# Wide attention on one core: another order of TensorE's work within a pair of heads, and one value projection of the next batch in every pair

## The reference, cut to what matters

```python
def _L2_attn_ref(x, Wq, Wk, Wv, Wo, bo):
    q, k, v = (x @ Wq), (x @ Wk), (x @ Wv)            # each to (b, 512, 16, 64)
    bias = slope[:, None, None] * (pos[:, None] - pos[None, :])
    scores = jnp.einsum('bihd,bjhd->bhij', q, k) * scale + bias[None]
    scores = jnp.where(causal[None, None], scores, jnp.float32(-1e+30))
    attn = jax.nn.softmax(scores, axis=-1)
    out = jnp.einsum('bhij,bjhd->bihd', attn, v).reshape(b, n, H * DH)
    return out @ Wo + bo
x = x + _L2_attn_ref(_layernorm(x, axis=-1), ...)
```

## Time and profile before

| | us |
|---|---|
| profiled execution, its own time | 3037.45 |
| its span on the core | 3035.5 |
| median of the runs | 3040.95 |
| TensorE busy | 2375.1 (78%) |
| VectorE busy | 2067.0 (68%) |
| ScalarE busy | 1820.5 (60%) |
| mean granted TensorE clock | 0.867 of 2.4 GHz |

### The profile page before, as it was taken

How to read it: one execution, slowest core, us unless ns; L and a number is a source line. 1 busy time by engine, 2 the same in 40 slices (tenths; PEclk the granted TensorE clock), 3 DMA queues, 4 the chain that set the end, 5 groups by cost and what they waited for, 6 DMA issues and landing times. The chain is left out here.

```text
span 3035.5 us, 44101 instructions
## 1 busy us (share of the span) xinstructions
PE 2375.1 (78%) x13097; PEld 1228.9 (40%) x13097; DVE 2067.0 (68%) x5951; ACT 1820.5 (60%) x4643; POOL 928.2 (31%) x1192
## 2 busy tenths in 40 slices
PE   4645574828888878289999999996767888888887
PEld 4434443612222246244444444443523444444452
DVE  4516651659999947656666666665558999999855
ACT  2111213317777763167677667774438999999964
POOL 2640166254344332200000000000454444444336
PEclk7776676558999975589999999998788999999979
DMA  6320232022424200000000000000011111111000
GB/s 178 70 48 0 84 61 46 1 37 49 77 48 76 51 8 0 29 1 1 1 1 1 1 1 1 1 1 1 1 33 29 29 29 29 29 29 22 8 1 28
DMA packets 230435, 86.72 MB, mean 29 GB/s; under 512 B 175234, under 2 KB 223298, under 8 KB 230210
## 3 DMA queue, kind: packets, MB, share of 16 engines
q1 hardware_dynamic: 215298, 71.60, 11.4%
q0 software_dynamic: 9856, 7.58, 1.9%
q10 hardware_dynamic: 5056, 4.83, 0.6%
HBM read 26.53 MB, written 15.50 MB: 14 GB/s over the span
## 5 line engine op out<-in xcount | busy, mean ns | idle before, releaser
L2183 ACT ACTIVATE s_pT<-s_ps_t 128x512 f32<-128x512 f32 x1024 | 626.5, 639 | 142.6 <-PE s_ps_t L1783 124.9
L1936 DVE TENSOR_REDUCE s_neg_max<-s_ps_a 128x1 f32<-128x512 f32 x1024 | 666.6, 682 | 64.9 <-PE s_ps_a L1749 55.1
L2174 ACT ACTIVATE s_first<-s_ps_a,s_neg_max 128x512 f32<-128x512 f32 x512 | 391.8, 765 | 25.2 <-DVE s_neg_max L1936 23.8
L1795 PE MATMUL s_ps_t<-ident,s_first 128*128 128x128 f32 x2048 | 316.8, 285 | 83.6 <-ACT s_pT L2183 70.8
L2592 ACT ACTIVATE s_e<-s_e,s_neg_max 128x128 f32<-128x128 f32 (+3 forms) x512 | 283.2, 555 | 164.9 <-DVE s_neg_max L2492 162.6
L139 POOL TENSOR_TENSOR s_rstd<-s_ve,minus_half 128x4 f32<-128x4 f32 x48 | 50.6, 1054 | 1001.5 <-DVE s_ve L126 1000.8
L2105 POOL TENSOR_SCALAR s_first<-s_first,s_rec 128x512 f32<-128x512 f32 x128 | 232.5, 1816 | 368.3 <-DVE s_rec L1942 362.4
L2492 DVE CUSTOM_DVE_ANT_0 s_e<-s_ps_a,w_alibi 128x128 f32<-128x128 f32 (+3 forms) x512 | 230.5, 488 | 113.7 <-PE s_ps_a L2362 113.7
L1749 PE MATMUL s_ps_a<-s_lanesT 64*128 64x512 bf16 x1024 | 274.9, 400 | 40.1 <-DMA s_lanesT<-n_lanes 23.4
L1795 PEld LDWEIGHTS s_ps_t<-ident,s_first 128*128 128x128 f32 x2048 | 220.9, 142 | 183.3 <-ACT s_pT L2183 142.0
L1810 PE MATMUL s_ps_o<-s_pT,n_v_pad 128*32 128x512 f32 x2048 | 277.6, 616 | 12.0 <-ACT s_oT L2189 12.0
(11 more groups left out here) (378 smaller groups left out, 4041.2 us busy)
## 6 DMA issues: line engine op xcount, KB each, us to landing
s_token_rows<-s_rows SPq DMA_DIRECT2D x4, 1088.0 KB, 5.4
s_x_rows<-x SPq DMA_DIRECT2D x4, 1024.0 KB, 5.3
x<-s_x_rows SPq DMA_DIRECT2D x8, 512.0 KB, 6.1
s_Wi<-L_ffn_experts_inter SPq DMA_DIRECT2D x2, 1792.0 KB, 8.4
x<-L_attn_x SPq DMA_DIRECT2D x4, 512.0 KB, 10.1
out<-x SPq DMA_DIRECT2D x4, 512.0 KB, 5.3
s_lanesT<-n_lanes SPq DMA_TRANSPOSE x64, 5.0
s_shiftedT<-n_lanes SPq DMA_TRANSPOSE x64, 2.4
```

The lines of the kernel that those rows point to most:

```text
L1795: last = pe.transpose(st[n % NK][:, t * P:(t + 1) * P], first[:, p % NF, 2 * t + a, i * P:(i + 1) * P], G.ident[:])
L1936: dve.tensor_reduce(neg_max[:, column(n):column(n) + 1], sa[n % NA][:], AX.X, ALU.max, negate=True).then_inc(s.max_ready, 1)
L2174: act.activation(first[:, g % NF, n % PU, :], sa[n % NA][:], ACT.Exp, bias=neg_max[:, n:n + 1], accum_out=sum1[:, n % (NR * PU):n % (NR * ...
L2183: act.activation(pT[:, n % NP, :], st[n % NK][:], ACT.Exp).then_inc(s.probs_ready, 1)
```

## The change

The order within a pair is written out anew on TensorE, VectorE and ScalarE. No instruction of TensorE is added or taken away; what changes is what stands beside what, and in which pair. On TensorE a pair is now:

```diff
+                    by_keys(g, 0)
+                    if further:
+                        project_q(g + LAG + 1)
+                    if ahead:
+                        scores(g + LAG, 0)
+                    if g:
+                        products(g - 1, TB - 1)
+                    products(g, 0)
+                    if ahead:
+                        scores(g + LAG, 1)
+                    by_keys(g, 1)
+                    if further:
+                        project_k(g + LAG + 1)
+                    by_keys(g, 2)
+                    if r == 1 and j:
+                        out_T(j - 1)
+                    if r == 5 and j + 2 < B:
+                        norm_T(j + 1)
+                    if ahead:
+                        scores(g + LAG, 2)
+                    products(g, 1)
+                    products(g, 2)
+                    if ahead:
+                        scores(g + LAG, 3)
+                    by_keys(g, 3)
+                    if g:
+                        output(g - 1)
+                    if j + 1 < B:
+                        v_product(g)
```

Each of the first 56 pairs has one `v_product`. The waits follow:

```diff
@@ project_q
-                        if r >= 4 and jp + 1 < B:
-                            pe.wait_ge(s.v_copied, 2 * TB * jp + 2 * (r - 4) + 2)
+                    if before >= 0:
+                        pe.wait_ge(s.v_copied, min(before + 1, 2 * TB * (B - 1)))
@@ v_product
+                    j, r = divmod(n, PB)
+                    pe.wait_ge(s.k_ready, n + LAG + 2)
+                    pe.wait_ge(s.xnT_ready, j + 2)
@@ norm_T
-                    if j >= 0:
-                        pe.wait_ge(s.k_ready, PB * j + 3 + LAG + 2)
+                    if j == 0:
+                        pe.wait_ge(s.k_ready, LAG + 1)
+                    if j > 0:
+                        pe.wait_ge(s.k_ready, PB * (j - 1) + 5 + LAG + 2)
```

```diff
 VectorE
+                    if g + 1 < PAIRS:
+                        invert(g + 1)
+                        normalise_probs(g + 1, 0)
+                        normalise_probs(g + 1, 1)
+                    if ahead:
+                        bias_and_maximum(g + LAG, 0)
+                    if g + 1 < PAIRS:
+                        normalise_probs(g + 1, 2)
+                    if ahead:
+                        bias_and_maximum(g + LAG, 1)
+                    if g + 1 < PAIRS:
+                        normalise_probs(g + 1, 3)
+                    if g + LAG + 1 < PAIRS:
+                        copy_k(g + LAG + 1)
+                    if r == 1 and j:
+                        add_to_x(j - 1)
+                    if ahead:
+                        bias_and_maximum(g + LAG, 2)
...
+                    if ahead:
+                        bias_and_maximum(g + LAG, 3)
+                    if r == 4 and j + 2 < B:
+                        normalise(j + 2)
+                    if j + 1 < B:
+                        copy_v(g)
 ScalarE
+                    if r == 1 and j:
+                        copy_out(j - 1)
+                    copy_probs(g, 0)
+                    if g + LAG + 1 < PAIRS:
+                        copy_q(g + LAG + 1)
+                    if ahead:
+                        exps(g + LAG, 0)
+                    copy_probs(g, 1)
+                    if ahead:
+                        exps(g + LAG, 1)
+                    copy_probs(g, 2)
+                    if g:
+                        copy_pair(g - 1)
+                    if r == 5 and j + 2 < B:
+                        copy_xnT(j + 2)
+                    if ahead:
+                        exps(g + LAG, 2)
+                    copy_probs(g, 3)
+                    if ahead:
+                        exps(g + LAG, 3)
```

More of the change, by code:

```diff
@@ L2331, in project_q @@
                     j, pair = divmod(g, PB)
-                    jp, r = divmod(g - LAG - 2, PB)
+                    before = g - LAG - 2
+                    jp, r = divmod(before, PB)
                     if g:
                         pe.wait_ge(s.k_ready, g)
-                    if g >= LAG + 2:
+                    if before == -1:
+                        pe.wait_ge(s.xnT_ready, 2)
+                    if before >= 0:
+                        pe.wait_ge(s.v_copied, min(before + 1, 2 * TB * (B - 1)))
                         if r == 1 and jp:
                             pe.wait_ge(s.x_added, jp)
-                        if r == 3 and jp + 1 < B:
-                            pe.wait_ge(s.xnT_ready, jp + 2)
-                        if r >= 4 and jp + 1 < B:
-                            pe.wait_ge(s.v_copied, 2 * TB * jp + 2 * (r - 4) + 2)
                     if j and pair == 0:
@@ L2400, in v_product @@
                 def v_product(n):
+                    j, r = divmod(n, PB)
+                    pe.wait_ge(s.k_ready, n + LAG + 2)
+                    pe.wait_ge(s.xnT_ready, j + 2)
+                    if r == 1 and j:
+                        pe.wait_ge(s.x_added, j)
+                    if r == 5 and j + 2 < B:
+                        pe.wait_ge(s.xnT_ready, j + 3)
                     t, half = n % (2 * TB) // 2, n % 2
@@ L2440, in _ @@
                             scores(g, t)
+                norm_T(0)
                 pe.wait_ge(s.v_first, 2 * TB)
@@ L2443, in _ @@
                     j, r = divmod(g, PB)
[L2444 to L2469, removed]
@@ new lines, in _ @@
+                    ahead, further = g + LAG < PAIRS, g + LAG + 1 < PAIRS
+                    by_keys(g, 0)
[11 more added lines that the diff above has]
+                        project_k(g + LAG + 1)
@@ L2538, in _ @@
                 normalise(0)
+                statistics(1)
+                N.aggregate(dve, do)
                 for g in range(LAG + 1):
                     copy_k(g)
+                    if g == 0:
+                        normalise(1)
                     if g < LAG:
@@ L2548, in _ @@
                     j, r = divmod(g, PB)
[L2549 to L2570, removed]
+                    ahead = g + LAG < PAIRS
@@ new lines, in _ @@
+                    if g + LAG + 1 < PAIRS:
[4 more added lines that the diff above has]
+                        bias_and_maximum(g + LAG, 2)
+                    if j + 2 < B:
+                        if r == 3:
+                            dve.wait_ge(s.xn_ready, TB * (j + 2))
+                            statistics(j + 2)
+                        if r == 4:
+                            N.aggregate(dve, do)
@@ L2642, in _ @@
                 copy_q(2)
+                copy_xnT(1)
                 for g in range(PAIRS):
                     j, r = divmod(g, PB)
[L2645 to L2656, removed]
+                    ahead = g + LAG < PAIRS
+                    if r == 1 and j:
+                        copy_out(j - 1)
[10 more added lines that the diff above has]
+                        copy_pair(g - 1)
+                    if r == 5 and j + 2 < B:
+                        copy_xnT(j + 2)
[4 more added lines that the diff above has]
+                        exps(g + LAG, 3)
                 copy_pair(PAIRS - 1)
```

## The result

| | before | after |
|---|---|---|
| median, us | 3039.35 (4 runs, 3035.01 to 3044.19) | 3011.89 (4 runs, 3008.47 to 3014.28) |
| span of the profiled execution | 3035.5 | 3008.7 |

The ratio is 0.991, 95% interval 0.9895 to 0.9926: faster by 0.9%, 27.5 us. The prediction was 3011, with 30 us saved from its median.

The account below looks back on a forecast made before the run. TensorE's own sequence bounds it: fewer changes of kind, less new waits, take the 56 pairs from 684.4 to 653.9 us; 30 saved in all gives 3007 profiled, 3011 with 3.5 added for the median. Own range 3003 to 3027.

Parts of the forecast that it names:

- The joints: TensorE's changes between kinds of work: 0.70 us a round, two rounds 1.40, so a plain pair takes 10.46.
- `project_q` behind `copy_v`: At the pair's seam TensorE waits 0.07 us, plus 0.10 for a late weight load: 0.17 per value-projection pair, giving 11.49.
- `out_T` and `norm_T`: Transposes behind project_k: 0.51 us wait, 0.05 entry and 0.44 work, 1.00 each, 13 times in the stretch.
- `normalise` at r = 4: On VectorE, between its last maximum and copy_v: delays the copy about 0.26 us, 6 times.
- Scores 3: Behind the maximum of scores 2, second head: needs 2.04 us against 2.08 of TensorE's work; no wait, no room.
- The ends: Outside the 56 pairs: four pairs ahead +0.6 us, pair behind saves 0.7, last three 0, before the loop 0.
- A: Rival: no new wait, the bank passes in time everywhere; 16 us more saved, 2995; chance 0.08.
- B: Rival: fewer changes between kinds but reloads stay; a pair saves 0.39 instead of 0.75, 3034 us; chance 0.10.
- the estimate of 14 us from the Trainium skill's drain: TensorE's mode changes at 0.053 us each, 12 against 8 a pair: 14 us saved before any new wait.
- C: Rival: copy_v comes late at the misc bank and all TensorE stands; 1.6 us behind gives 3058; chance 0.05.

Follow-up runs that it names:

- half-apart run: The changed kernel with products(g-1, 3) ahead of scores 0, in the first round only; 3020.99 us, ratio 0.9945.
- the spread alone: The old four slots on all engines, with one value projection in slot 3 of every pair and the layer norm one batch earlier; 3037.34 us, ratio 1.000.
- The run with one wait: The changed kernel without project_q's wait for copy_k where its wait for copy_v already implies it; 3011.95 us.
- the late copy: The changed kernel with copy_v moved on VectorE behind the next invert and normalise_probs(g+1, 0); 3056.54 us, ratio 1.0068.

## Why the prediction was right, step by step

The mechanism was right: fewer joints, less a wait for the bank at the seam. That 3011 came within 1 us of 3011.89 is partly luck. The profiled execution was put at 3007 and took 3010.49. The pairs and the end of the layer cost some 7 us more than forecast; 3.1 us came in that nobody had reckoned with, 1.7 at the entry and 1.4 ahead of the layer. And the median lies 1.4 above the profiled execution, where 3.5 had been added.

- **The joints.** Right in every term: leave 0.10, entry at a transpose 0.05, products side by side free, full products behind transposes free. The plain pair was put at 10.46; the last plain pair measures 10.48 or 10.49 in the changed kernel and in all those made from it that leave the products side by side. One joint by itself is shown by the half-apart run, their sum by the spread alone, which has none fewer and gains nothing.
- **`project_q` behind `copy_v`.** Right in mechanism, too small: 0.24 in place of 0.17. The step took 0.05 from the copy's end to the matmul from a row in which the product has one wait; this one has two, and takes 0.14. The run with one wait shows the difference. The wait was 0.16 for 0.07, the late load 0.08 for 0.10. A pair is 11.58 against 11.49, 4.7 us over 52 pairs, and that is the error of the stretch: the 56 pairs were put at 653.9 and took 658.7, as the errors of the next two terms nearly cancel.
- **`out_T` and `norm_T`.** Put at 1.00 each, measured 1.06 and 1.05 (12.64 and 12.63 less 11.58): 0.60 of wait before the transposes for 0.51 and 0.05. `norm_T` too has two waits, and 0.15 from the copy's end to its start; no run takes one of them away here, so that the second wait does it is argued only.
- **`normalise` at r = 4.** Put at 0.26, measured 0.10 (11.68 less 11.58) in the changed kernel. VectorE's last maximum is done when it was reckoned, 0.20 behind the start of `v_product` (1664.32 and 1664.12 in the trace), but the four instructions hold VectorE for 1.02, not 1.15, so the copy starts at 1665.34, 0.16 late and not 0.30.
- **Scores 3.** "No wait, and no room" was right, and mattered: a kernel that takes 0.65 from that distance waits 0.61, as the 0.04 of room has it.
- **The ends.** The four pairs ahead of the stretch were put at a loss of 0.6 and lost 1.4 (46.76 us for 45.34). The entry before them was put at 0 and gained 1.7 (36.12 for 37.83), of which the clock may have its part: the spread of the entry above is larger than that. Behind the stretch 0.7 was to be saved and 0.8 is lost (37.22 us to the layer's last transposes, for 36.43): there TensorE waits for ScalarE's `copy_probs` six times, 2.4 us in all, where it waited twice, 1.3 us. So the 0 for the last three pairs came from a wait wrongly taken to be equal in both orders. 1.4 us of the difference in spans lie ahead of the layer's first `project_q` (1286.99 for 1288.44) and are not the change's: over all ten kernels' profiles that point moves between 1283.2 and 1288.7.
- **The rivals.** A (no wait) is what `v_product` ahead of `output` gives for the bank alone. B, and with it the estimate of 14 us from the Trainium skill's drain ("TensorE: Matmul & The Clock Gate", Part 2), is refuted: a change of kind costs 0.10 to leave, twice 53 ns, and 0.05 to 0.10 more in the first weight reload. C (slower) is what the late copy gives. The Trainium skill's rule that a change of mode drains the engine ("TensorEngine Tiling (Array Packing)", Key Properties) agrees with the rows: 0.09 to 0.10 at each change of kind, nothing between full products and transposes or between two products groups, where the mode stays.

## What to carry to other kernels

When one engine is busy throughout, lay its instructions end to end and price the joints by kind: here 0.15 to 0.20 us for each of twelve in a pair of 12 us, and reordering took a third of them away with no work removed. Then follow each shared bank around the new order, for the gain brings fill and reuse nearer to each other: 0.86 us of independent work put between them was worth another 12 us, and 0.8 us of delay at the same place turned the gain into a loss. A distance that the ledger calls just enough is to be kept in mind at the next edit.

## What the runs showed of the hardware

- Two column-tiled products groups beside each other run with no gap and no exposed weight load (1.23 us for 1.08 of work, with one entry and one leave in it), while the same group behind another kind pays 0.05 of reload and 0.10 on leaving.
- A late wait costs twice: its own length, and the next weight load. Behind transposes `project_q` spans 1.10 to 1.12 after a wait and 1.02 without. Its weights are not loaded ahead: the load starts with the release, in the row above 0.11 us behind the copy's end. The Trainium skill ("TensorE: Matmul & The Clock Gate", Part 2) says that weight loads are pulled ahead of matmuls in flight; the trace shows that for a product that needn't wait (`v_product`, 0.43 us ahead), not for these.
- With two waits ahead of `project_q` the late one costs about 0.07 us a pair more than with one (11.58 and 11.51).
